# Reading out linear attention with the state held still and q streamed, q divided beforehand

## The reference, cut to what matters

```python
xn = layernorm(x)                                  # x: 8 x 1024 x 256, float32
q, k = elu(heads(xn @ Wq.T)) + 1, elu(heads(xn @ Wk.T)) + 1     # 16 heads of 16
v = heads(xn @ Wv.T)
kv_state = einsum('bhnd,bhne->bhde', k, v)
k_state = k.sum(axis=2)
attn = einsum('bhnd,bhde->bhne', q, kv_state)
denom = maximum(einsum('bhnd,bhd->bhn', q, k_state), 1e-06)
attn = attn / denom
local = three-tap convolution of xn along the sequence, per channel, + conv_b
out = x + (attn + local) @ Wp.T + bp + ffn(xn)     # ffn: silu(gate) * up, down; 256 -> 768 -> 256
```

## Time and profile before

| | us |
|---|---|
| median of three runs | 505.0 |
| the profiled execution | 504.68 |
| its span in the profile | 503.0 |
| around the span | 1.7 |
| TensorE busy | 490.9 (98%) |
| VectorE busy | 429.3 (85%) |
| ScalarE busy | 332.9 (66%) |

### The profile page before, as it was taken

One profiled execution on the slowest core, in us unless ns is written; L12 is line 12 of the kernel. 1 busy time (PEld: TensorE's weight loads), 2 busy tenths in 40 slices (PEclk: granted clock), 3 DMA queues, 4 the chain that ended last, 5 costly groups with the idle time before them and its releaser, 6 DMA issues.

```text
span 503.0 us, 11007 instructions
## 1 busy us (share of the span) xinstructions
PE 490.9 (98%) x3957; PEld 305.2 (61%) x3957; DVE 429.3 (85%) x827; ACT 332.9 (66%) x522; POOL 145.8 (29%) x162
## 2 busy tenths in 40 slices
PE   7989998999999999999999999999999999999997
PEld 6545364755657475574756657475565747657576
DVE  6797998889888888888889888889988889897787
ACT  1878857667485666748577585767748567674771
POOL 4476034140501414032140502314041141401050
PEclk9999999999999999999999999999999999999999
DMA  8637332343335324252342325233342432234012
GB/s 300 192 46 166 64 106 42 86 111 56 130 44 142 69 47 132 44 155 42 100 108 42 125 42 167 42 83 106 53 133 42 129 79 42 86 50 76 3 42 85
DMA packets 68669, 45.36 MB, mean 90 GB/s; under 512 B 33440, under 2 KB 68128, under 8 KB 68640
## 3 DMA queue, kind: packets, MB, share of 16 engines
q1 hardware_dynamic: 59232, 35.66, 25.5%
q0 software_dynamic: 8448, 8.39, 11.1%
q10 hardware_dynamic: 960, 0.92, 0.5%
HBM read 20.32 MB, written 8.39 MB: 57 GB/s over the span
## 4 chain that ended last, share of the span: by engine, by line
PE 86%; DVE 8%; ACT 3%; issue 2%; POOL 0%; DVEq 0%; POOLq 0%; ACTq 0%
PE ps L1126 16%; PE ps L1285 15%; PE ps L1304 15%; PE ps L1294 14%; PE ps L1228 14%; PE ps L1184 5%; PE ps L1193 3%; PE ps L1247 2%; DVE hid L975 1%; DVE hl L981 1%; PE ps L1134 1%; DVE local L904 1%; PE ps L1169 1%; ACT hh L590 1%; DVE p_wl L745 1%
## 5 line engine op out<-in xcount | busy, mean ns | idle before, releaser
L582 ACT ACTIVATE act_g<-ps,scales 128x512 f32<-128x512 f32 x96 | 66.0, 687 | 42.0 <-PE ps L1294 40.0
L975 DVE SCALAR_TENSOR_TENSOR hid<-act_g,scales,ps 128x512 f32<-128x512 f32 x96 | 71.4, 744 | 21.3 <-ACT act_g L582 20.7
L981 DVE TENSOR_TENSOR hl<-hid,hh 128x512 f16<-128x512 f32 x96 | 66.7, 694 | 2.2 <-ACT hh L590 0.8
L365 POOL TENSOR_TENSOR xT<-xh,xl 128x1024 f32<-128x1024 f16 x15 | 31.8, 2122 | 112.5 <-issue 98.1
L590 ACT ACTIVATE hh<-hid 128x512 f16<-128x512 f32 x96 | 59.7, 622 | 5.4 <-DVE hid L975 5.4
L1285 PE MATMUL ps<-xh,g_wh 128*128 128x512 f16 x192 | 57.6, 382 | 2.1 <-DVE q_relu L930 1.2
L1294 PE MATMUL ps<-xl,g_wh 128*128 128x512 f16 x192 | 57.1, 379 | 0.0
L1294 PE MATMUL ps<-xl,u_wh 128*128 128x512 f16 x192 | 57.1, 379 | 0.0
L1285 PE MATMUL ps<-xh,u_wh 128*128 128x512 f16 x192 | 57.1, 379 | 0.0
L1304 PE MATMUL ps<-d_wh,hh 128*128 128x256 f16 x384 | 52.5, 273 | 1.3 <-DVE hid L975 1.3
L330 POOL TENSOR_SCALAR xn<-x_in,neg_mean,rstd 128x256 f32<-128x256 f32 x62 | 52.3, 857 | 4.3 <-POOL rstd L337 4.2
(11 more groups left out here) (162 smaller groups left out, 964.7 us busy)
## 6 DMA issues: line engine op xcount, KB each, us to landing
xb<-bp_sb SPq DMA_DIRECT2D x16, 512.0 KB, 3.3
xb<-in_L_attn_x_dram POOLq DMA_DIRECT2D x16, 512.0 KB, 5.9
x_in<-in_L_attn_x_dram SPq DMA_DIRECT2D x15, 512.0 KB, 4.2
out_dram<-out_sb SPq DMA_DIRECT2D x14, 512.0 KB, 2.9
wg_int<-in_L_ffn_w_gate_dram SPq DMA_DIRECT2D x1, 768.0 KB, 6.9
wu_int<-in_L_ffn_w_up_dram SPq DMA_DIRECT2D x1, 768.0 KB, 8.4
wd_int<-in_L_ffn_w_down_dram SPq DMA_DIRECT2D x1, 768.0 KB, 11.2
out_dram<-out_sb SPq DMA_DIRECT2D x3, 256.0 KB, 2.1
```

The source lines that it names most:

```text
L582: nc.scalar.activation(act_g[:, j % 2, :], ps[:, gate_bank(j), :], ACT.Silu, scale=silu_in).then_inc(silu_ready, 1)
L975: nc.vector.scalar_tensor_tensor(out=hid[:, j % 2, :], in0=act_g[:, j % 2, :], scalar=h_mul, in1=ps[:, gate_bank(j) + 1, :], op0=ALU.mult, ...
L981: nc.vector.tensor_tensor(hl[:, j, :], hid[:, j % 2, :], hh[:, j, :], ALU.subtract).then_inc(hl_ready, 1)
```

## The change

- `query` and `transpose_attn` go. The state (`state`, now without the eight columns) is held still and q is streamed: `numerators`, two float32 products of 512 columns, whose result has channels on partitions already. It needs q divided beforehand.
- The denominators come from `denominators`: four float32 products with `key_sums` (32 stationary columns, of which eight are used) held still and 256 tokens of q streamed, each on its own column tile, into one bank. A head is a partition of the result, a token a column.
- `divide_one` on VectorE clips 256 columns and takes 256 reciprocals a partition. `spread_den` on SyncE's queue copies them by four DMAs from SBUF to SBUF, each from 8 partitions to 128 (every row 16 times, 128 KB each), to `over_den`. `divide_q` on VectorE multiplies q by it, 1024 columns.
- TensorE's order: `denominators` stands where `query` stood, `gate_up(0)` between the two `accumulate`, and `numerators` behind `gate_up(1)`. Two waits go: that of `query` on `acc_kept`, and that of `accumulate(0)` on `attn_ready`.
- VectorE's order: `divide_one` stands for the two `normalise`, `divide_q` for the two `put_y` behind `relu_q`; `put_y` twice now stands behind `hidden_low(0)`, and `put_q` behind `hidden_low(4)`, ahead of `hidden_low(5)`.
- SyncE's queue: the four spreading DMAs stand first in the step, ahead of the load of x_in.
- The last step has a new order on VectorE and TensorE, and new banks.

```diff
+            def spread_den(b, c):
+                sp.wait_ge(den_inv, at(b, c, 1, 1))
+                for k in range(KT):
+                    for h in range(2):
+                        rows = slice((2 * k + h) * GROUP, (2 * k + h) * GROUP + HPB)
+                        sp.dma_start(over_den[:, c, k, h * DEN_TOKENS:(h + 1) * DEN_TOKENS],
+                                     rden[rows, c, :].unsqueeze(1).broadcast_to([HPB, HD, DEN_TOKENS])
+                                     ).then_inc(den_spread[c], 16)
...
             def step(b, c, attend, ahead):
+                if attend:
+                    spread_den(b - 1, c)
...
+            def divide_one(b, c, bank):
+                dve.wait_ge(den_done, at(b, c, 1, 1))
...
+                nc.vector.tensor_scalar(den[:, :], ps[:, bank, 0:DEN_TOKENS], 1e-6, None, ALU.max).then_inc(den_kept, 1)
...
+                nc.vector.reciprocal(rden[:, c, :], den[:, :]).then_inc(den_inv, 1)
+
+            def divide_q(b, c):
+                dve.wait_ge(den_spread[c], b * 64 + 64)
+                nc.vector.tensor_tensor(q_sb[:, c, :, :], q_sb[:, c, :, :], over_den[:, c, :, :],
+                                        ALU.mult).then_inc(q_divided, 1)
...
                 if attend:
-                    normalise(b - 1, c, 0, QKV)
-                    normalise(b - 1, c, 1, QKV)
+                    divide_one(b - 1, c, DEN)
                     put_k(0)
...
                     relu_q()
-                    put_y(b - 1, c, 0, TURNED)
-                    put_y(b - 1, c, 1, TURNED)
+                    divide_q(b - 1, c)
                 if ahead:
                     for j in range(J):
                         hidden(j)
-                        if j == 0 and attend:
-                            put_q(b, c)
...
                         if j >= 1:
                             hidden_low(j - 1)
+                        if j == 1 and attend:
+                            put_y(b - 1, c, 0, NUM)
+                            put_y(b - 1, c, 1, NUM)
+                        if j == 5 and attend:
+                            put_q(b, c)
...
+            def denominators(b, c, bank):
...
+                for k in range(KT):
+                    for h in range(2):
+                        g = (2 * k + h) * GROUP
+                        ins = nc.tensor.matmul(ps[g:g + GROUP, bank, 0:DEN_TOKENS], key_sums[:, side_of(b), k, :],
+                                               q_sb[:, c, k, h * DEN_TOKENS:(h + 1) * DEN_TOKENS], start=True, stop=True,
+                                               tile_position=(0, g))
+                ins.then_inc(den_done, 1)
+
+            def numerators(b, c, banks):
+                pe.wait_ge(q_divided, at(b, c, 1, 1))
+                for k in range(KT):
+                    ins = nc.tensor.matmul(ps[:, banks[k], :], state[:, side_of(b), k, :], q_sb[:, c, k, :], start=True, stop=True)
+                ins.then_inc(num_done, 1)
```

More of the change, by code:

```diff
@@ L59, in at, with side_of @@
         return b * (CB * per_step) + (c * per_step + k)
+    def side_of(b):
+        return 1 if isinstance(b, int) and b == NB - 1 else 0
     with ExitStack() as ctx:
@@ L166, in build @@
         DOWN = [gate_bank(J - 2), 7]
[L168 to L171 removed]
+        LAST_DEN = [STATE, 7]
+        LAST_NUM = [[6, 7], [2, 3]]
+        LAST_WP = [[0, 1], [6, 7]]
+        LAST_DOWN = [4, 5]
         def halves(bank):
@@ L294, in step @@
             def step(b, c, attend, ahead):
+                if attend:
+                    spread_den(b - 1, c)
+                if not ahead:
+                    spread_den(b, 0)
+                    spread_den(b, 1)
                 if not (isinstance(b, int) and b == NB - 1):
@@ L626, in step @@
                         hidden_high(j - 1)
-                    if attend and j == (Y_SPLIT[0] if ahead else 0):
+                    if attend and j == Y_SPLIT[0]:
                         y_high(b - 1, c, 0)
-                    if attend and j == (Y_SPLIT[1] if ahead else 1):
+                    if attend and j == Y_SPLIT[1]:
                         y_high(b - 1, c, 1)
@@ L867, in put_y @@
                     dve.wait_ge(wp_done, at(b, c, 2, p - 1))
-                nc.vector.scalar_tensor_tensor(out=y[:, :, cols], in0=halves(banks[p]), scalar=attn_to_y,
+                both = ps[:, banks[0]:banks[1] + 1, cols]
+                nc.vector.scalar_tensor_tensor(out=y[:, :, cols], in0=both, scalar=attn_to_y,
                                                in1=local[:, :, c * CHUNK + p * PAIR:c * CHUNK + (p + 1) * PAIR],
@@ L1051, in step @@
                         hidden(j)
-                        if j == 0 and attend:
-                            put_q(b, c)
-                        elif j == 0:
+                        if j == 0 and not attend:
                             put_first_q()
@@ L1239, in accumulate @@
                         pe.wait_ge(acc_kept, at(b, c, 1, 0))
-                    if p == 0 and attend:
-                        pe.wait_ge(attn_ready, at(b - 1, c, 2, 2))
                     for i in (2 * p, 2 * p + 1):
@@ L1369, in step @@
                     pe.wait_ge(res_ready, at(b, c - 1, 2, 2))
-                    pe.wait_ge(acc_kept, at(b, c, 1, 0))
-                    query(b - 1, c, 0, QKV)
-                    query(b - 1, c, 1, QKV)
+                    denominators(b - 1, c, DEN)
                 project_kv(1)
@@ L1375, in step @@
                 accumulate(0)
+                gate_up(0)
+                accumulate(1)
+                gate_up(1)
                 if attend:
-                    transpose_attn(b - 1, c, 0, TURNED)
-                    transpose_attn(b - 1, c, 1, TURNED)
-                accumulate(1)
-                gate_up(0)
-                gate_up(1)
+                    numerators(b - 1, c, NUM)
                 if isinstance(b, int) and b == 1 and c == 0:
@@ L1403, in step @@
                 else:
-                    first, second = 0, 1
                     gate_up(2)
+                    denominators(b, 0, LAST_DEN[0])
+                    gate_up(3)
+                    denominators(b, 1, LAST_DEN[1])
+                    gate_up(4)
                     project_y(b - 1, c, 0, WP)
-                    gate_up(3)
+                    gate_up(5)
                     project_y(b - 1, c, 1, WP)
-                    gate_up(4)
-                    pe.wait_ge(out_ready, at(b - 1, c, 2, 2))
-                    query(b, first, 0, LAST_QKV[0])
-                    query(b, first, 1, LAST_QKV[0])
-                    gate_up(5)
-                    pe.wait_ge(hid_ready, at(b, c, J, J - 1))
-                    query(b, second, 0, LAST_QKV[1])
-                    transpose_attn(b, first, 0, LAST_YT[0])
-                    pe.wait_ge(hid_ready, at(b, c, J, J))
-                    query(b, second, 1, LAST_QKV[1])
-                    transpose_attn(b, first, 1, LAST_YT[0])
-                    down(0, LAST_DOWN)
-                    project_y(b, first, 0, LAST_WP[0])
-                    project_y(b, first, 1, LAST_WP[0])
-                    transpose_attn(b, second, 0, LAST_YT[1])
-                    transpose_attn(b, second, 1, LAST_YT[1])
+                    numerators(b, 0, LAST_NUM[0])
+                    pe.wait_ge(hid_ready, at(b, c, J, J))
+                    pe.wait_ge(out_ready, at(b - 1, c, 2, 1))
+                    down(0, LAST_DOWN)
+                    numerators(b, 1, LAST_NUM[1])
+                    project_y(b, 0, 0, LAST_WP[0])
+                    project_y(b, 0, 1, LAST_WP[0])
+                    pe.wait_ge(out_ready, at(b - 1, c, 2, 2))
                     down(1, LAST_DOWN)
-                    project_y(b, second, 0, LAST_WP[1])
-                    project_y(b, second, 1, LAST_WP[1])
+                    project_y(b, 1, 0, LAST_WP[1])
+                    project_y(b, 1, 1, LAST_WP[1])
             is_wide = {}
```

104 lines of the change are left out of this document (40 added, 64 removed).

## The result

The changed kernel takes 694.1 us (691.97 to 697.79) against 505.0 us (504.65 to 505.31) of the kernel before: a ratio of 1.375, with a 95% interval of 1.369 to 1.381. The forecast was 508 us with a range of 503 to 535; the direction was right, the size was not, by 186 us. The mechanism of most of it was on the list, as rival (a), with 630 us and a chance of 0.13.

The account below looks back on a forecast made before the run. TensorE, busy 98%, was taken to bound the kernel, with VectorE second at 85%. From 504.7 us, -0.5 over 13 steps and +3.8 in the last step gave 508.0 us; range 503 to 535.

Parts of the forecast that it names:

- rival (a): Spreading DMAs reading 8 of 128 partitions get 47 GB/s; TensorE waits 8.2 us a step, about 630 us; chance 0.13.
- The products: TensorE in each step: query and transposes, 2.87 us, go; numerators and denominators, 2.35 us, come.
- Rival (b): Denominators' column tiles on TensorE don't overlap for 256 columns: 1.3 us more a step, 528 us; chance 0.05.
- the stall on hl of block 5: End of step: put_q ahead of hidden_low(5) makes TensorE wait 0.43 us in down(0).
- the 0.52 us a step: TensorE's pure products of a step: 2.87 us less, 2.35 us more, 0.52 us saved.
- VectorE's load: VectorE gets 3.4 us instead of 2.6 a step; reciprocal of 256 columns 1.74 us, reciprocals ready at 6.9 us.
- the landing of the spread: Four DMAs behind the reciprocals land 10.7 to 12.3 us into a step, taken as 11.7: 0.1 us waiting.
- The clock: TensorE's clock behind the last step's 4.6 us wait: nothing in the sum, up to 2 us in the range.
- the forecast of +3: Whole kernel with a punctual spread: -0.5 us over 13 steps and +3.8 us in the last step.
- The last step: VectorE's new order makes TensorE wait 4.6 us ahead of the numerators of (7, 0): +3.8 us.
- the forecast was 0.04: A common step: -0.52 products, +0.43 hl, -0.09 small waits, +0.04 gate_up(1), +0.1 landing: -0.04 us.

Follow-up runs that it names:

- with the wait fed: The changed kernel with 40 unread float32 products on TensorE inside the wait, ahead of each numerators but those of the last two chunks: 670.2 us.
- the kernel with both ends reordered: Kernel with four columns, put_q behind put_state (514.4 us), with the last step reordered and put_q(0, 1) one step earlier: 510.5 us, 1.011.
- with four columns: The changed kernel with key_sums holding each head's column four times, so each spreading DMA reads 32 neighbouring rows 4 times each: 521.9 us, 1.033.
- the mended kernel: By its step times of 30.0 us, the kernel with both ends reordered: 510.5 us, 1.011.

## Why the prediction was wrong, point by point

**Where the 187 us are.** Spans of the profiled executions, in the order in which the causes come off: changed kernel 690.4; with the wait fed 665.4, so the clock takes 25.0; without the spread 517.5, so waiting for it takes 147.9; and 14.5 us remain to the 503.0 of before, for the order (with what the clock costs in its first attending and its last step). The steps say the same: 13 from start to start take 554.2 us in the changed kernel, 530.6 with the wait fed and 397.8 without the spread.

**The products: right.** The denominators, bounded by 0.44 and 1.91 and taken as 0.61, take 0.57 us (start to start below), the numerators at full clock 1.72 or 1.82, forecast 1.74. TensorE of the changed kernel, around the end of a step and the start of the next:

```profile
362.88 0.38 PE L1323 MATMUL ps<-d_wh,hl 128*128 128x256 f16 x2
363.46 0.39 PE L1323 MATMUL ps<-d_wh,hl 128*128 128x256 f16 x2 [0.19 <-DVE hl L1001]
...
366.30 1.03 PE L1250 MATMUL ps<-kv_wh,xh 128*128 128x512 f16 x4
...
368.99 0.64 PE L1207 MATMUL ps<-q_sb,key_sums 128*32 128x256 f32 x8
369.56 0.82 PE L1250 MATMUL ps<-kv_wh,xh 128*128 128x512 f16 x3
```

Rival (b) is out. (The first two lines are the stall on hl of block 5: 0.58 us from start to start, 0.36 more than the 0.22 of the pair.) Not all of the 0.52 us a step arrives: of the kernel with both ends reordered the steps (b, 0) take 30.0 us and the steps (b, 1), but for (2, 1), 29.5 to 29.7, those of before 30.0 and 29.8. In them the two `accumulate`, each now between products of another shape, take 0.98 with their changeovers instead of 0.88, the first `project_kv` with the changeover behind it 2.68 instead of 2.59, the numerators 1.82.

**VectorE's load: right, its timing in half of the steps.** The reciprocal of 256 columns takes 1.75 us, extrapolated as 1.74 from 4 and 32 columns, and `divide_q` 1.22. The reciprocals are ready 6.9 us into the steps (b, 1), as forecast, and 8.3 us into the steps (b, 0), as in (4, 0) (330.94 - 322.65). There VectorE starts late, since the product that writes `key_sums` has met GpSimd's addition:

```profile
319.97 2.35 POOL L387 TENSOR_TENSOR xT<-xh,xl 128x1024 f32<-128x1024 f16 x1 [27.52 <-issue]
...
320.25 2.10 DVE L984 TENSOR_TENSOR key_sums<-whole_acc,head_mask 128x16 f32<-128x16 f32 x1
```

**The step that failed: the landing of the spread.** The prediction bounded it between 1.7 us (a 128 KB store) and 3.3 us (a 512 KB fill) behind the last of four issues of 0.70 each: at most 5.4 us behind the reciprocals. It was 14.7. Both bounding rows are transfers out of all 128 partitions, and the size was carried over while the shape of the source was not. With a source on 32 neighbours the same bound does hold, with 4.7 us in the step shown. The text named the gap ("no row shows a transfer slowed by its source; that is weak, since none has a narrow source") and then let the weak argument give it 0.13. A bound from rows that don't share the property in question is no bound.

**Rival (a), right in kind.** Its rate, an eighth of 377 GB/s and so 47, is the 44 of the trace, but its 630 us are 64 short: the wait is 10.2 us a step ((530.6 - 397.8) / 13) instead of 8.2, 26 in all, the clock 25, and the order 11 more than its 3. Of the 2.0 us a step that the wait is longer, 1.8 are the landing: 14.7 us behind the reciprocals, where the rival's sum has 12.9.

**The clock: left out.** The prediction had "nothing in the sum, up to 2 us in the range" for what a wait does to the clock. In the last step of the kernel without a spread TensorE waits 5.39 us (forecast 4.6) and the numerators then take 3.4 us; so a term of 1.7 us there, which the 2 us of the range cover, and of 1.8 on the mean of the 13 steps, most of which have a wait of 10 us, for which the range had nothing.

```profile
498.28 3.58 PE L1208 MATMUL ps<-q_sb,state 128*128 128x512 f32 x4 [5.39 <-DVE q_sb L864]
```

**The order: mis-sized, and by things not on the list.** Without the spread the forecast of +3 was +14.3. In that run every second common step takes 30.9 instead of 30.0 us, 5.4 in six steps. That this is the collision with GpSimd is read from another kernel: taking it away with four columns gave 7.6. The first attending step takes 34.1 instead of 31.5, as gate_up(1) waits 2.85 us for q_relu: put_q(0, 1) stands ahead of it, and TensorE now asks earlier. Behind this wait the clock is at 0.50 again, and gate_up(1) takes 3.16 us instead of 1.73.

```profile
82.19 1.03 PE L1296 MATMUL ps<-xh,g_wh 128*128 128x512 f16 x2 [2.85 <-DVE q_relu L941]
```

The last step takes 6.6 more (51.6 against 45.0) instead of 3.8; GpSimd's additions and the clock, taken away in a better order, were 3.1. The other six common steps are 0.1 shorter each. Together 5.4 + 2.6 + 6.6 - 0.5 = 14.1. The stall on hl of block 5, worked out to 0.43 us a step, is 0.36, and taking it away is worth some 0.1, since another wait stands behind it. The twelve common steps with `put_q` behind `put_state` are 29.85 us on the mean, 0.05 shorter than before. That the forecast was 0.04 is luck: it has 0.43 us for hl in it, which isn't paid in this order, so by its terms these steps should have been some 0.4 us shorter still. One slip of the sum is small: the terms of the last step as listed make 29.2 us, not 29.4.

**What stays open.** With GpSimd's additions away the last step still takes 48.6 us, 3.6 more than before, for a chain of reciprocal, spread and `divide_q` that the old order didn't have; whether an order exists that hides it is not known. Also why the steps (b, 0) of the mended kernel take 30.0 us and not 29.6, as the steps (b, 1) do, and why step (2, 1) takes 30.5 to 30.8 in every kernel with four columns: its spread lands 5.7 us behind the reciprocals instead of 4.7, and TensorE waits 0.8 to 1.0 us for it.

## What to carry to other kernels

Cost a DMA by how many groups of neighbouring partitions its source is laid over, before its bytes (every destination here was all 128, so nothing is shown for that side), and look at what its queue can issue. If a few rows have to be spread over all partitions, compute them in several copies or on spaced partitions (here the products had the columns to spare), which took 172 us off for no work. And when an instruction of VectorE with both inputs in SBUF is moved, look which instruction of GpSimd runs at the new time; when TensorE is made to wait for several us, add what it loses behind the wait at half clock.

## What the hardware showed that was not expected

- A DMA out of 8 neighbouring partitions of SBUF moves 44 GB/s, out of the same number of rows on every second one 93, with the rest alike. The issues behind it on its queue get longer too: each of the four took 1.55 us instead of 0.6, the load of x_in behind them 2.79 instead of 0.4.
- The granted clock fell to 0.50 within waits of TensorE of 5 to 10 us and stayed there behind them, for 5 us of dense products in the step shown. In the last steps here it also fell where the waits were 0.90, 1.76 and 0.73 us with products between them, and did not where they were 0.54, 0.76 and 0.73, nor where they were 0.53 and 1.81.
- A float32 reciprocal on VectorE keeps to 6.2 ns a column from 4 to 256 columns (0.18 to 1.75 us).
- A 0.42 us product of VectorE took 2.2 us beside an addition of GpSimd, and in another kernel GpSimd's addition took 2.8 instead of 2.1 us beside VectorE's `put_q`, which had started 0.4 us ahead of it: in these rows the one that starts second pays.
